# Four of 32 edge tiles picked by one-hot matmuls instead of gathered, in four passes of a four-layer graph network

## The reference

```python
def _step(embedding, src, dst, etype, W_msg, b_msg, ...):
    m = (embedding @ W_msg.T + b_msg).reshape(n, N_EDGE_TYPES, DIM)
    q = m[src, etype]
    r = jax.ops.segment_sum(q, dst, num_segments=n)
    return _gru_cell(r, embedding, w_ih, w_hh, b_ih, b_hh)
```

## Time and profile before

| | |
|---|---|
| median of 3 runs | 5234.55 us (5216.54 to 5239.27) |
| profiled execution, device time | 5233.15 us |
| its span | 5231.4 us |
| mean granted clock of TensorE | 0.665 |
| indirect gathers (GpSimd) | 2912, 2803 us busy |
| stretches of the seven gather passes | 597, 597, 599, 607, 659, 603 and 671 us |

### The profile page before, as it was taken

The page is one execution under the profiler, slowest core; times in us unless marked ns, Lnnn a source line. Parts: engine busy times, 40 slices in busy tenths (PEclk is TensorE's granted clock), DMA queues, the critical chain, the costliest instruction groups (busy, mean ns, idle before and its releaser), DMA issues.

```text
span 5231.4 us, 42580 instructions
## 1 busy us (share of the span) xinstructions
PE 2481.9 (47%) x12006; PEld 2039.6 (39%) x12007; DVE 1519.5 (29%) x3455; ACT 424.8 (8%) x692; POOL 2834.5 (54%) x2944
## 2 busy tenths in 40 slices
PE   5223363233522336444466656652333655555387
PEld 3222232222322333443345555532322445544374
DVE  3111141111411114222242222211111555555874
ACT  1000010000100001000010000110000100000133
POOL 3666636666466664666635665346666355554000
PEclk8556575555755567555567887865566766666699
DMA  4111121111211112111111111111111233333140
GB/s 158 47 44 47 45 76 47 46 45 44 77 47 46 45 44 78 46 45 46 44 31 40 42 42 39 27 41 45 47 46 42 68 114 121 121 121 106 49 148 25
DMA packets 146356, 318.40 MB, mean 61 GB/s; under 512 B 51123, under 2 KB 65658, under 8 KB 145786
## 3 DMA queue, kind: packets, MB, share of 16 engines
q0 software_dynamic: 99840, 218.29, 15.9%
q1 hardware_dynamic: 46458, 99.48, 5.4%
HBM read 255.94 MB, written 61.63 MB: 61 GB/s over the span
## 4 chain that ended last, share of the span: by engine, by line
another core or an unknown queue 17%; PE 13%; DVE 10%; issue 7%; DVEq 1%; POOL 1%; ACT 1%; DMA 0%; ACTq 0%
PE ps L1266 12%; DVE oh L815 2%; DVE small L1065 1%; DVE ring L1055 1%; DVE ring L1062 1%; DVE ring L983 1%; DVE pw L1056 1%; POOL ring L431 0%; DVEq L815 0%; POOL small L441 0%; PE ps L1380 0%; DVE ring L1097 0%; DVE ring L1144 0%; DVE nodes L1098 0%
## 5 line engine op out<-in xcount | busy, mean ns | idle before, releaser
L431 POOL DMA_INDIRECT ring<-m_tab,idx x1664 | 1606.8, 966 | 1003.2 <-issue 487.5
L1266 PE MATMUL ps<-oh,ring 128*128 128x128 f32 x5824 | 1236.9, 388 | 1906.5 <-DVE oh L815 1082.3
L1266 PEld LDWEIGHTS ps<-oh,ring 128*128 128x128 f32 x5824 | 1129.0, 286 | 1987.1 <-issue 1963.5
L815 DVE TENSOR_TENSOR oh<-cst,dl 128x256 f32<-128x256 f32 x1664 | 591.6, 419 | 2582.5 <-remote 2146.8
L431 POOL DMA_INDIRECT ring<-x_tab,idx x832 | 797.3, 958 | 462.3 <-issue 237.0
L431 POOL DMA_INDIRECT ring<-kv_tab,idx x416 | 399.2, 960 | 288.8 <-DVE rec L1070 147.4
L441 POOL TENSOR_TENSOR small<-small,bc 128x4 f32<-128x4 f32 (+1 forms) x28 | 31.0, 1109 | 635.9 <-DVE small L906 635.9
L1266 PE MATMUL ps<-wpad,rts 128*128 128x128 f32 x832 | 180.8, 360 | 261.0 <-issue 191.8
L1266 PEld LDWEIGHTS ps<-wpad,rts 128*128 128x128 f32 x832 | 149.1, 256 | 292.9 <-issue 220.3
L1266 PE MATMUL ps<-nodes,wt 128*128 128x512 f32 (+1 forms) x532 | 237.6, 588 | 36.1 <-DVE nodes L840 11.2
L494 ACT ACTIVATE nodes<-ps 128x512 f32<-128x512 f32 x18 | 9.4, 597 | 2924.5 <-PE ps L1266 2924.5
(11 more groups left out here) (233 smaller groups left out, 1999.3 us busy)
## 6 DMA issues: line engine op xcount, KB each, us to landing
ring<-m_tab,idx POOLq DMA_INDIRECT x1664
ve_dr<-pw SPq DMA_DIRECT2D x52, 512.0 KB
ring<-ve_dr SPq DMA_DIRECT2D x52, 512.0 KB, 3.4
m_tab<-ring SPq DMA_DIRECT2D x75, 256.0 KB, 2.1
ring<-x_tab,idx POOLq DMA_INDIRECT x832
ring<-kv_tab,idx POOLq DMA_INDIRECT x416
m_tab<-oh SPq DMA_DIRECT2D x25, 256.0 KB, 2.1
nodes<-in_xT SPq DMA_DIRECT2D x2, 1600.0 KB, 10.3
```

The source lines that it names most:

```text
L431: pool.indirect_dma_start(ring[:, u, j, 0:width], None, table, bass.IndirectOffsetOnAxis(ap=idx[:, g * WV + j:g * WV + j + 1], axis=0)).th ...
L815: ins = V.tensor_tensor(oh[:, v, j:j + 2, :], iota.unsqueeze(1).to_broadcast([P, 2, P]), dl[:, ds((i * RING + (u + ahead)) * WV + j, 2)].u ...
L1266: return T.matmul(o, lhsT, rhs, start=start, stop=stop, skip_group_check=True)
```

## The change

In the first three steps of L0 and in L2, the last four tiles of each turn (wave 3, slots 4 to 7) are not gathered. TensorE picks them out of the node table in SBUF:

- Once a pass (`split_nodes`): the node table is turned back to node by partition and split in three bf16 pieces whose sum is the f32 value (`pieces`, in recT's room).
- Once a turn: SyncE loads the four tiles' 512 source numbers, repeated on all partitions (`src_row`, 256 KB written, in wpad's room). For each of the 25 windows ScalarE makes a selector of 128 x 512 (`selectors`): Square of (source - node number), then Relu of (1 - that), a bf16 one-hot. There are two `dist` and five `sel` buffers. TensorE multiplies each with the window's three pieces, all adding in bank 7 (`pick`): nine windows after wave 0, sixteen after wave 1. ScalarE copies the result out (`pickT`).
- In wave 2, after each two tiles' sums, TensorE turns one picked tile back: in L0 by a matmul with the four types' message weights, plus a bf16 matmul with the bias; VectorE then masks by type (`maskG`) and adds the four (`picked_by_type`). In L2 it is a transpose, and VectorE copies the four tiles at once (`picked`). The rows go to the ring's slots 4 to 7 of wave 3.
- recT and wpad are written to or read again from HBM: recT is stored once at the start (ScalarE waits for it ahead of the first pass), and both are loaded before L1 and before L3.

The gathers' waits count with the fewer landings (`landed`). The core of the diff, indented less:

```diff
+GS = 4
+G_FROM = RING * WV - GS
+GPASS = STEPS - 1
+SBUFS = 5
+AHEAD = 2 * WIN
+BY_AC = range(WIN)
+G_PARTS = [range(0, 9), range(9, 18), range(18, WIN)]
+PARTS = 3
...
+    sp.wait_ge(s_ac, AC["srcT"])
+    turned = pw[:, 1, :].rearrange("p (b e) -> p b e", b=4)
+    whole = SLOTS // P
+    sp.dma_start(src_dr[0:whole * P, :].rearrange("(b s) e -> s b e", s=P),
+                 turned[:, 0:whole, :]).then_inc(g_store, 16)
+    sp.dma_start(src_dr[whole * P:SLOTS, :], turned[0:SLOTS - whole * P, whole, :]).then_inc(g_store, 16)
+    sp.wait_ge(s_ac, AC[f"recT{WAVES // 4 - 1}"])
+    sp.dma_start(recT_dr, recT[:, :]).then_inc(g_spill, 16)
+    sp.wait_ge(g_store, 32)
+    sp.wait_ge(g_spill, 16)
+    def src_rows(r):
+        with sp.Fori(0, TURNS) as i:
+            sp.wait_ge(g_used, (r * TURNS + i) * WIN + AHEAD)
+            row = src_dr[ds(i * (RING * WV) + G_FROM, GS), :].rearrange("(a s) e -> a (s e)", a=1)
+            sp.dma_start(src_row, row.to_broadcast([P, GS * P])).then_inc(g_row, 16)
+    def restore(r):
+        sp.wait_ge(g_used, r * (TURNS * WIN) + AHEAD)
+        sp.dma_start(recT[:, :], recT_dr).then_inc(g_back, 16)
+        sp.dma_start(wpad_f, a["wpad"]).then_inc(g_back, 16)
             with sp.Fori(0, STEPS - 1) as s:
+        src_rows(s)
                 table(s + 1, m_rows, 512)
+    restore(GPASS)
...
+    src_rows(GPASS)
+    restore(GPASS + 1)
...
-            for j in range(WV):
+            for j in range(WV - GS if selects(k) and u == RING - 1 else WV):
...
+    def split_nodes(g):
+        def middle(c):
+            cw = CH[c][1]
+            act.wait_ge(tb_r1, g * NCH + (c + 1))
+            n0, n1 = CH[c][0] // P, (CH[c][0] + cw) // P
+            nc.scalar.activation(pieces[:, n0:n1, 1, :],
+                                 dist[:, c % 2, 0:cw].rearrange("p (w d) -> p w d", d=D),
+                                 ACT.Copy).then_inc(tb_mid, 1)
+        for c, (c0, cw) in enumerate(CH):
+            act.wait_ge(tb_mm, g * NCH + (c + 1))
+            nc.scalar.activation(pieces[:, c0 // P:(c0 + cw) // P, 0, :],
+                                 ps[:, c, 0:cw].rearrange("p (w d) -> p w d", d=D),
+                                 ACT.Copy).then_inc(tb_hi, 1)
+            if c >= 1:
+                middle(c - 1)
+        middle(NCH - 1)
+        act.wait_ge(tb_lo, (g + 1) * NCH)
...
+    def selectors(g, i):
+        for n, w_ in enumerate(BY_AC):
+            b = n % 2
+            if n == 0:
+                act.wait_ge(g_row, (g * TURNS + i + 1) * 16)
+            nc.scalar.activation(dist[:, b, :], src_row, ACT.Square,
+                                 bias=node_m[:, w_:w_ + 1]).then_inc(g_dist, 1)
+            act.wait_ge(g_dist, (g * TURNS + i) * WIN + (n + 1))
+            act.wait_ge(g_used, (g * TURNS + i) * WIN + (w_ - SBUFS + 1 + AHEAD))
+            nc.scalar.activation(sel[:, w_ % SBUFS, :], dist[:, b, :], ACT.Relu, scale=-1.0,
+                                 bias=ones[:, 0:1]).then_inc(g_sa, 1)
+        act.wait_ge(g_used, (g * TURNS + i + 1) * WIN + AHEAD)
+        nc.scalar.activation(pickT, ps[:, 7, :], ACT.Copy).then_inc(g_pick, 1)
...
+    act.wait_ge(g_spill, 16)
+    act.wait_ge(s_dv, DV["g_init"])
             with act.Fori(0, STEPS - 1) as s:
                 hidden(s, "L0")
+        split_nodes(s)
+        with act.Fori(0, TURNS) as i:
+            selectors(s, i)
...
+    def split_nodes(g):
+        def low(c):
+            cw = CH[c][1]
+            n0, n1 = CH[c][0] // P, (CH[c][0] + cw) // P
+            dve.wait_ge(tb_mid, g * NCH + (c + 1))
+            V.tensor_tensor(pieces[:, n0:n1, 2, :], dist[:, c % 2, 0:cw].rearrange("p (w d) -> p w d", d=D),
+                            pieces[:, n0:n1, 1, :], ALU.subtract).then_inc(tb_lo, 1)
+        for c, (c0, cw) in enumerate(CH):
+            n0, n1 = c0 // P, (c0 + cw) // P
+            dve.wait_ge(tb_hi, g * NCH + (c + 1))
+            if c >= 2:
+                low(c - 2)
+                dve.wait_ge(tb_lo, g * NCH + (c - 1))
+            V.tensor_tensor(dist[:, c % 2, 0:cw].rearrange("p (w d) -> p w d", d=D),
+                            ps[:, c, 0:cw].rearrange("p (w d) -> p w d", d=D), pieces[:, n0:n1, 0, :],
+                            ALU.subtract).then_inc(tb_r1, 1)
+        for c in (NCH - 2, NCH - 1):
+            low(c)
+    def picked_by_type(g, i):
+        for j in range(GS):
+            n = (g * TURNS + i) * GS + j
+            dve.wait_ge(g_tr, n + 1)
+            dve.wait_ge(g_slot, n + GS)
+            V.tensor_tensor(typed.rearrange("p (t d) -> p t d", d=D),
+                            ps[:, 7, :].rearrange("p (t d) -> p t d", d=D),
+                            maskG[:, ds(i * GS + j, 1), :].rearrange("p a t -> p (a t)").unsqueeze(2)
+                            .to_broadcast([P, ET, D]), ALU.mult).then_inc(g_typed, 1)
+            dve.wait_ge(g_typed, n + 1)
+            V.tensor_reduce(ring[:, RING - 1, WV - GS + j, 0:D], typed.rearrange("p (t d) -> p d t", d=D),
+                            AX.X, ALU.add).then_inc(g_slot, 1)
+    def picked(g, i):
+        dve.wait_ge(g_tr, (GPASS * TURNS + i) * GS + GS)
+        V.tensor_copy(ring[:, RING - 1, WV - GS:WV, 0:D],
+                      ps[:, 7, :].rearrange("p (s d) -> p s d", d=D)).then_inc(g_slot, GS)
+    def sums_by_two(k, g, pick):
+        split_nodes(g)
+        with dve.Fori(0, TURNS) as i:
+            for u in range(RING):
+                dve.wait_ge(credit, wave_no(k, i, u) + 3)
+                one_hot(k, i, u).then_inc(oh_ready, 1)
+            pick(g, i)
...
+    def split_nodes(g, h):
+        for c, (c0, cw) in enumerate(CH):
+            for j in range(cw // P):
+                ins = T.transpose(ps[:, c, j * P:(j + 1) * P], h[:, c0 + j * P:c0 + (j + 1) * P], ident)
+            ins.then_inc(tb_mm, 1)
+        pe.wait_ge(tb_r1, (g + 1) * NCH)
+    def pick(g, i, ws):
+        for w_ in ws:
+            if w_ == 0:
+                pe.wait_ge(tb_lo, (g + 1) * NCH)
+            pe.wait_ge(g_sa, (g * TURNS + i) * WIN + (w_ + 1))
+            for k in range(PARTS):
+                ins = mm(ps[:, 7, :], pieces[:, w_, k, :], sel[:, w_ % SBUFS, :], start=(w_ + k == 0),
+                         stop=(w_ == WIN - 1 and k == PARTS - 1))
+            ins.then_inc(g_used, 1)
+    def turned_by_type(g, i, j):
+        n = (g * TURNS + i) * GS + j
+        if j:
+            pe.wait_ge(g_typed, n)
+        mm(ps[:, 7, :], pickT[:, j * P:(j + 1) * P], w("L0_WmsgT", 0, 4), stop=False)
+        mm(ps[:, 7, :], ones_b[0:PARTS, :], bias_b[0:PARTS, :], start=False).then_inc(g_tr, 1)
+    def turned(g, i, j):
+        ins = T.transpose(ps[:, 7, j * P:(j + 1) * P], pickT[:, j * P:(j + 1) * P], ident)
+        if j == GS - 1:
+            ins.then_inc(g_tr, GS)
+    def sums_by_two(k, g, turn):
+        with pe.Fori(0, TURNS) as i:
+            for u in range(RING):
+                cs = load_cols(pe, cols, i, u)
+                pe.wait_ge(gat[u], landed(k, u, i))
+                pe.wait_ge(oh_ready, oh_no(k, i, u))
+                for j in range(WV):
+                    if u == 2 and j % 2 == 0:
+                        if j == 0:
+                            pe.wait_ge(g_pick, g * TURNS + i + 1)
+                        turn(g, i, j // 2)
+                    if u == RING - 1 and j == WV - GS:
+                        pe.wait_ge(g_slot, (g * TURNS + i + 2) * GS)
+                    ins = mm(psf[:, ds(cs[j], P)], ring[:, u, j, 0:D], oh[:, u % 2, j, :], start=False,
+                             stop=False)
+                ins.then_inc(credit, 1)
+                if u == 0:
+                    pick(g, i, G_PARTS[0])
+                if u == 1:
+                    pick(g, i, G_PARTS[1])
+                    pick(g, i, G_PARTS[2])
```

115 lines of the change are left out of this document (103 added, 12 removed).

## The result

The changed kernel takes 6083.82 us (median of 4 runs, 6072.87 to 6111.16) against 5236.91 us before: ratio 1.163, 95% interval 1.158 to 1.169. The forecast was 5415 us, its range 5190 to 5720. Slower was right; +847 us in place of +183 is outside the range. The profiled execution took 6091.77 us (span 6089.7, clock 0.79 in place of 0.665).

The account below looks back on a forecast made before the run. No engine was near full; GpSimd's gathers came nearest (54%), setting a turn's floor. Three L0 passes +156, L2 +3 and the spill +24 made +183 us on 5233.15 us: 5415 us, range 5190 to 5720.

Parts of the forecast that it names:

- Selector: ScalarE's Square and Relu for one window: 1.49 us each, 37.3 us for the 25 of a turn.
- TensorE's prices: Matmul times at 2.4 GHz: 0.7 us for a selector's three, 0.90 and 0.24 us for turning back a picked tile.
- bare circles: Turn of mutual waits between ScalarE, TensorE and VectorE at 2.4 GHz: 45.6 us in L0, 41.0 in L2.
- Clock: TensorE's granted clock in the picking passes: 0.89, so 22% of the time at 1.2 GHz; turns 48.1 and 42.2 us.
- low-clock rival: TensorE stays at 1.2 GHz in the picking passes: +573 us, 5805 us in all; chance 0.12.
- Start of a pass: Splitting the node table, then the first turn's selectors without lead: last used 58 us after an L0 pass's first gather.
- Spill: Storing recT to HBM ahead of the first pass: 22 us, +24 with its landing; 12 to 45 possible.
- Sum without late reports: Whole change: +156 us for three L0 passes, +3 for L2, +24 for the spill, +183 in all.
- The step that failed: GpSimd's turn with 28 gathers and its pauses, 40.2 us, lies below ScalarE and TensorE's 48.1 in L0, 42.2 in L2.
- late releases land on the new circle: Rival: TensorE's late releases exceed the five selector buffers' cover, 6.1 us a turn, 317 more, 5730 us; chance 0.14.
- cheap selectors: Rival: Relu follows Square without a gap, 1.22 us a selector at 2.4 GHz, turn 40.4 us, 5080 us; chance 0.18.
- Signs of the after-profile: Expected in L0: turns of 48 us, GpSimd waiting 8 us or more for TensorE, Squares 1.49 us apart, clock near 0.89.

Follow-up runs that it names:

- e4_plain: Changed kernel with every indirect gather of the picking passes replaced by a plain DMA of the same size from GpSimd's queue; output not the reference's; 5264.88 us.
- v3: Changed kernel with four GpSimd memsets before each wave in the picking passes, three in L1, and a wait for landed gathers in L3; 5240.98 us, ratio 0.9995.
- e7_paced: Changed kernel with plain DMAs in place of the picking passes' gathers and a GpSimd memset after each; output not the reference's; 5299.10 us.
- e5_busy: Changed kernel with four memsets of GpSimd's own ahead of each wave of gathers in the picking passes; 5391.10 us.
- v2: Kernel before, with three GpSimd memsets ahead of every wave in L1 and a wait for landed gathers ahead of every wave in L3; 5116.79 us, ratio 0.9775.
- e1_pause: Changed kernel with GpSimd waiting, before each wave's gathers in the picking passes, until its previous wave's gathers have landed; 5450.49 us, ratio 1.039.
- b2_pauses: Kernel before, with GpSimd waiting for its gathers to land ahead of every wave in L1 and L3, every second in L0 and L2; 5155.72 us, ratio 0.987.

## Why the prediction was wrong, step by step

- **Selector.** Forecast 1.49 us; Relus start 1.44 us apart when releases come (738.00, 739.44). Right.
- **TensorE's prices.** Three pick matmuls take 0.82 us at the high level, forecast 0.7; typed turns every 2.42 us (VectorE's products in pass 0 at 704.93 and 707.35), forecast 2.07: their two matmuls took 1.12 and 0.39 us, not 0.90 and 0.24. Right in sum: the bare circles are 45.3 and 40.7 us against 45.6 and 41.0.
- **Clock.** Forecast 0.89. The changed kernel has 0.86 in pass 0 and 0.81 in L2, but as a result of the late reports: 1.00 in e4_plain's turn and 0.98 in v3's pass 0. So that 0.86 is near 0.89 is luck. The 2.5 us a turn (1.2 in L2) that the forecast added for a low clock, 110 of its 183 us, are not there when the reports come in time, and the low-clock rival falls. That the clock dropped where TensorE waited for selectors agrees with what the Trainium skill (TensorE: Matmul & The Clock Gate, section HAM oscillation) says of short bursts with waits; it was an effect here, not the cause.
- **Start of a pass.** Forecast 58 us from first gather to the last selector used. In e7_paced the first DMA of pass 1 is at 738.7 and the copy at 796.2, 57.5 us: right without late reports. In the changed kernel it is 82.
- **Spill.** Forecast 24 us, lower bound 12. In e7_paced the same distance in pass 0 is 128.0 - 56.5 = 71.5, so 14. The spill itself landed in 13.9 us in e4_plain's list of DMAs. Too high by 10: 1600 KB in 10.3 us was a poor guide for 3392 KB.
- **Sum without late reports.** +183 forecast. e5_busy, where a few are left, shows +158 of span, v3 against v2 +124. e4_plain, where none are left in the passes that pick, shows +31, and in those four passes +33 (33, 16 and 20 in L0, -36 in L2), where the forecast's lower edge, the turn at 2.4 GHz throughout, had +73. So even without the failed step the forecast was too high, by the clock, the spill and L2.
- **The step that failed** is the sentence that GpSimd's 40.2 us is below both circles, "so nothing is left of its gain but slack". The pauses in that 40.2 were taken as a cost of GpSimd alone, covered by the slack. They are a delay of TensorE's reports, and an engine that waits closely for TensorE pays it: in place of the 48.1 us a turn took 61.1, and 48.8 in e1_pause and 45.3 in e4_plain, where the reports come mostly or wholly in time. Before, GpSimd waited with four waves of cover (40 us of gathers) and VectorE's one-hots with two; the change hung 25 releases a turn on the same reports with a cover of five selectors (7.2 us).
- **The rival "late releases land on the new circle"** was this mechanism, at a chance of 0.14 and a price too small by half. It took the 6.1 us that GpSimd stood in L3, which is what the cover left over. The delays themselves stood in the earlier trace rows: 15.44, 28.08 and 19.34 us. The last less the 7.5 us of the five buffers is 12 us a turn; measured were 61.1 - 48.8 = 12.3 with e1_pause taking it away, 15.8 against e4_plain. That it fits so well is hindsight: the other two would have given 8 and 21. At 13 us the rival gives 5415 + 52 x 13, some 6090, close to the 6084 measured; but that number is in part luck, since the 48.1 us under it holds a clock term that the runs without late reports do not show. Its argument against itself, that the waits thin out when gathers pause, was half true: they do, but the gathers' rows of 20 between pauses were long enough.
- **The range.** Its upper end, 5720, lay under this rival's own time, 5730. So it left out not only most of the low clock and half of the cheap selectors, as it says, but all of the late releases: by the prediction's own chances it held about 0.65, not 0.8.
- **Signs of the after-profile.** GpSimd waits of 8 us or more a turn came (19.45 us in one wait), selectors 1.44 us apart came for part of a turn only, and the turn of 48 us did not.

## What to carry to other kernels

When a profile shows a wait that it can't name, price it by its length at the engine that waits longest, not by what the best-covered waiter has left; then ask what cover each new waiter has. This kernel, which feeds TensorE from rows of indirect gathers on GpSimd, gained from short breaks in them (1.7 us or more of anything else after 8 gathers) where an engine waits closely on TensorE's results, and gained nothing where GpSimd is the bound (L0 in b2_pauses: 591 us of gathers, 587 before). Whether others do is worth one run. Before building a hand-over between ScalarE and TensorE 25 times a turn, test it beside the traffic that it will run in.
